# Front order of a Mamba-and-attention block on one core: attention output turned behind the output projection, norms on GpSimd, value copies on VectorE

## What is computed

```python
xn = _layernorm(x)
s = _L0_attn_ref(xn, ...)      # x + mamba2(layernorm(x)), then x + gelu MLP(layernorm(x))
g = _silu(_L0_ffn_ref(xn, ...))
return x + s * g
...
# _L0_ffn_ref, the part that matters here
h = _rms(x, n1_w)
q = _rms(heads(wq), qn_w); k = _rms(heads(wk), kn_w); v = heads(wv)     # 16 heads of 8
ao = softmax(causal(q k^T / sqrt(8))) @ v ... @ wo.T                    # first 32 channels set to 0
x = x + ao
xf = _rms(x, n2_w)                                                      # "second norm"
logits = nan_to_num(xf @ gate_w.T)                                      # 4 experts, the best 2 weighted
return x + weighted sum of four expert MLPs of xf
```

## Time and profile before

| | |
|---|---|
| median of 3 runs (range) | 860.65 us (860.46 to 865.01) |
| the profiled execution: time, span | 861.28 us, 859.5 us |
| granted TensorE clock, mean | 0.993 |
| TensorE matmuls / weight loads busy | 784.9 us (91%) / 482.5 us (56%) |
| VectorE busy | 618.1 us (72%) |
| ScalarE busy | 498.5 us (58%) |
| GpSimd busy | 320.8 us (37%) |

### The profile page before, as it was taken

The page is one execution under the profiler, slowest core; times in us unless marked ns, Lnnn a source line. Parts: engine busy times, 40 slices in busy tenths (PEclk is TensorE's granted clock), DMA queues, the critical chain, the costliest instruction groups (busy, mean ns, idle before and its releaser), DMA issues. The chain is left out here.

```text
span 859.5 us, 18101 instructions
## 1 busy us (share of the span) xinstructions
PE 784.9 (91%) x5472; PEld 482.5 (56%) x5472; DVE 618.1 (72%) x1469; ACT 498.5 (58%) x928; POOL 320.8 (37%) x600
## 2 busy tenths in 40 slices
PE   2779999998999989998999989999899998999897
PEld 1455564755557465665647555475556656475545
DVE  2786479785887768786697858877587876967534
ACT  2435784476753776457844767537764568447552
POOL 5424543053512717036340535227170362505400
PEclk9999999999999999999999999999999999999999
DMA  4000000000000000000000000000000000000000
GB/s 166 2 8 17 12 0 1 9 16 25 0 8 12 14 12 0 8 14 25 0 0 8 14 24 0 6 13 14 12 0 8 13 25 0 0 8 14 24 2 13
DMA packets 15145, 11.73 MB, mean 14 GB/s; under 512 B 1040, under 2 KB 13968, under 8 KB 14992
## 3 DMA queue, kind: packets, MB, share of 16 engines
q1 hardware_dynamic: 15120, 11.43, 4.4%
HBM read 7.76 MB, written 2.10 MB: 11 GB/s over the span
## 5 line engine op out<-in xcount | busy, mean ns | idle before, releaser
L1102 ACT ACTIVATE sb_pr<-S 128x768 f32<-128x768 f32 (+1 forms) x192 | 161.2, 878 | 135.0 <-PE S L445 134.9
L1198 DVE TENSOR_REDUCE sb_mx<-S 128x2 f32<-128x256 f32 (+3 forms) x256 | 198.0, 818 | 32.8 <-PE S L445 31.6
L1722 POOL TENSOR_SCALAR_AFFINE_SELECT sb_pr<-sb_pr 128x256 f32<-128x256 f32 (+1 forms) x192 | 98.8, 520 | 301.7 <-ACT sb_pr L1102 301.0
L445 PE MATMUL R<-sb_pr,sb_va 128*32 128x512 f32 (+3 forms) x1024 | 89.7, 445 | 6.3 <-POOL sb_pr L1722 6.3
L445 PE MATMUL R<-sb_W,sb_pr 128*128 128x96 f32 (+1 forms) x512 | 69.5, 276 | 0.0
L445 PE MATMUL R<-sb_xfT,sb_W 128*128 128x512 f32 x144 | 69.2, 602 | 0.0
L445 PE MATMUL S<-sb_kT,sb_qT 32*128 32x256 f32 (+3 forms) x512 | 56.0, 383 | 14.2 <-DVE sb_mx L1198 10.7
L445 PEld LDWEIGHTS R<-sb_W,sb_pr 128*128 128x128 f32 x512 | 63.5, 192 | 3.8 <-issue 3.5
L445 PEld LDWEIGHTS S<-sb_kT,sb_qT 32*128 32x128 f32 x512 | 27.4, 182 | 67.0 <-DVE sb_mx L1198 59.2
L1432 DVE SCALAR_TENSOR_TENSOR sb_x<-R,sb_wts,sb_x 128x96 f32<-128x96 f32 x128 | 40.6, 317 | 22.8 <-PE R L445 19.4
L445 PE MATMUL S<-sb_qT,sb_kT 32*128 32x256 f32 (+3 forms) x512 | 56.1, 383 | 0.5 <-ACT sb_pr L1102 0.5
(11 more groups left out here) (217 smaller groups left out, 1708.7 us busy)
## 6 DMA issues: line engine op xcount, KB each, us to landing
sb_xin<-x SPq DMA_DIRECT2D x9, 256.0 KB, 2.8
sb_W<-weights SPq DMA_DIRECT2D x1, 2290.0 KB, 11.6
sb_qT<-sb_mT SPq DMA_DIRECT2D x128, 4.0 KB
sb_xres<-x SPq DMA_DIRECT2D x8, 256.0 KB, 2.8
out<-sb_xres SPq DMA_DIRECT2D x7, 256.0 KB, 2.3
sb_cT<-sb_xact SPq DMA_DIRECT2D x8, 128.0 KB, 2.3
sb_W<-weights SPq DMA_DIRECT2D x1, 514.0 KB, 5.6
sb_cst<-consts SPq DMA_DIRECT2D x1, 328.0 KB, 3.1
```

The lines of the kernel that those rows point to most:

```text
L445: return pe.matmul(o, lhsT, rhs, start=start, stop=stop, skip_group_check=True)
L1102: act.activation(pr[:, e % 4, :, 0:n], S[pair_of_exp(e)][:, :, 0:n], ACT.Exp).then_inc(p_sb, 1)
L1198: o = dve.tensor_reduce(mx[:, n // P - 1, g, heads[0]:heads[1] + 1], found[:, :, at_col:at_col + n], AX.X, ALU.max, negate=True)
L1722: pool.affine_select(out=keep, in_=keep, compare_op=ALU.is_ge, fill=0.0, base=0, pattern=pattern, channel_multiplier=-1)\
```

## The change

On TensorE the first `qkv` projection moves to the end of `stage_a`, ahead of the last turn of y; the second goes in front of the output projection; the transposes of `ao` follow the output projection directly, then the third and fourth `qkv`, `wo`, and the x and z projections. The transposes of `xf` go behind all z projections, right ahead of the query and key transposes, and the gate's matmuls between the fourth and the fifth set of these.

On VectorE the value copies arrive (`evac_values`), two of them ahead of x1 and two behind; both norms leave; the sum of squares goes behind x2; the gate's six steps go between the second and the third key copy. On GpSimd both norms arrive: `first_norm` ahead of the multiply of the query weights, `second_norm` behind it. On ScalarE the value copies leave, the first norm's root comes earlier, the squares of x2 are taken in two halves, all z copies go ahead of `x1T` and `xfT`, and the first taps and the gate's exponential go behind the query copies. In the last front (tail alone) the orders stay the same but for the engine of the norms.

```diff
+            def project_qkv(r, t):
+                mm(bank(t)[:, 0:3 * D], xbT[:, t * P:(t + 1) * P], w("qkv")).then_inc(qkv_ps, 1)
+
+            def turn_second_norm(r):
+                pe.wait_ge(xf_sb, at(xf_sb, r, 1))
+                transposes(R[0], lambda t: xf[:, t, :]).then_inc(xfT_ps, 1)
+
+            def gate(r):
+                pe.wait_ge(xfT_sb, at(xfT_sb, r, 1))
+                pe.wait_ge(x1_sb, at(x1_sb, r, T))
+                for t in range(T):
+                    i = mm(R[2][:, t * E:(t + 1) * E], xfT[:, t * P:(t + 1) * P], w("gate"))
+                i.then_inc(gate_ps, 1)
...
+                if head:
+                    project_qkv(r, 1)
+                if tail:
...
                     i.then_inc(op_ps, 1)
-                if head:
-                    pe.wait_ge(xbT_sb, at(xbT_sb, r, 0))
-                    pe.wait_ge(p_sb, at(p_sb, r, 0))
-                    for t in range(T):
-                        mm(bank(t)[:, 0:3 * D], xbT[:, t * P:(t + 1) * P], w("qkv")).then_inc(qkv_ps, 1)
                 if tail:
                     pe.wait_ge(ao3_sb, at(ao3_sb, r, 2))
                     transposes(R[0], lambda t: ao[:, t, :]).then_inc(aoT_ps, 1)
...
                 if head:
-                    project_x(r, 0)
+                    project_qkv(r, 2)
+                    project_qkv(r, 3)
...
                 if head:
+                    project_x(r, 0)
                     project_x(r, 1)
                     project_z(r, 0)
-                    project_z(r, 1)
...
                 if head:
                     project_x(r, 2)
+                    project_z(r, 1)
                     project_z(r, 2)
-                if tail:
-                    pe.wait_ge(xf_sb, at(xf_sb, r, 1))
-                    transposes(R[0], lambda t: xf[:, t, :]).then_inc(xfT_ps, 1)
...
-                if head:
                     project_z(r, 3)
-                if tail:
-                    pe.wait_ge(xfT_sb, at(xfT_sb, r, 1))
-                    pe.wait_ge(x1_sb, at(x1_sb, r, T))
-                    for t in range(T):
-                        i = mm(R[2][:, t * E:(t + 1) * E], xfT[:, t * P:(t + 1) * P], w("gate"))
-                    i.then_inc(gate_ps, 1)
+                if tail and not head:
...
                 if head:
 
                     for n in range(2 * G):
+                        if tail and n == 0:
+                            turn_second_norm(r)
+                        if tail and n == T:
+                            gate(r)
                         if n == 0:
...
                 weigh_values(r, G * UNITS - 2)
+                pe.wait_ge(xbT_sb, at(xbT_sb, r, 1))
+                pe.wait_ge(p_sb, at(p_sb, r, G * UNITS))
+                project_qkv(r, 0)
                 turn_y(r, T - 1)
...
+            def evac_qkv(r, ts):
+                if 0 in ts:
+                    act.wait_ge(rn_sb, at(rn_sb, r, 0))
+                    act.wait_ge(lo_sb, at(lo_sb, r, 0))
+                    act.wait_ge(pv_ps, at(pv_ps, r, 0))
+                for t in ts:
                     act.wait_ge(qkv_ps, at(qkv_ps, r, t + 1))
                     act.activation(qk[:, t].rearrange("p a h d -> p (a h d)"), bank(t)[:, 0:2 * D], ACT.Copy,
-                                   scale=ratio[:, t:t + 1])
-                    act.activation(va[:, t, :, 0:HD],
-                                   bank(t)[:, 2 * D:3 * D].rearrange("p (h d) -> p h d", h=AH),
-                                   ACT.Copy, scale=ratio[:, t:t + 1]).then_inc(qkv_sb, 1)
+                                   scale=ratio[:, t:t + 1]).then_inc(qk_sb, 1)
...
                 if head:
-                    evac_qkv(r)
+                    evac_qkv(r, (0, 1))
                 if tail:
                     act.wait_ge(aoT_ps, at(aoT_ps, r, 1))
                     act.activation(aoT[:], R[0][:, :], ACT.Copy).then_inc(aoT_sb, 1)
                 if head:
-                    act.wait_ge(qkv_sb, at(qkv_sb, r, T))
+                    evac_qkv(r, (2, 3))
+                if head:
+                    act.wait_ge(qk_sb, at(qk_sb, r, T))
                     act.activation(sq[:], qk[:], ACT.Square).then_inc(sq_sb, 1)
+                if tail:
+                    act.wait_ge(ln2_sb, at(ln2_sb, r, 2))
+                    act.wait_ge(x1n_sb, at(x1n_sb, r, 0))
+                    inverse_root(r, mv2[:, :, 1], r2, r2_sb, 1.0, 0)
+                if head:
                     act.wait_ge(conv_dve, at(conv_dve, r, 0))
                     act.wait_ge(conv_pool, at(conv_pool, r, 0))
                     evac_xc(r, 0)
...
-                    inverse_root(r, mv2[:, :, 1], r2, r2_sb, 1.0, 0)
+                    act.wait_ge(x2_sb, at(x2_sb, r, 2))
+                    act.wait_ge(yss_sb, at(yss_sb, r, 0))
+                    for t in range(2):
+                        act.activation(junk[:, t // 2, t % 2 * D:t % 2 * D + D], x2[:, t, :], ACT.Square,
+                                       accum_out=x2ss[:, t:t + 1])
...
                 if tail:
-                    act.wait_ge(x2_sb, at(x2_sb, r, 2))
-                    act.wait_ge(yss_sb, at(yss_sb, r, 0))
-                    for t in range(T):
+                    for t in range(2, T):
                         i = act.activation(junk[:, t // 2, t % 2 * D:t % 2 * D + D], x2[:, t, :], ACT.Square,
                                            accum_out=x2ss[:, t:t + 1])
                     i.then_inc(x2ss_sb, 1)
...
                     evac_z(r, 0)
-                if tail:
-                    act.wait_ge(xfT_ps, at(xfT_ps, r, 1))
-                    act.activation(xfT[:], R[0][:, :], ACT.Copy,
-                                   scale=vec[:, V_N2W:V_N2W + 1]).then_inc(xfT_sb, 1)
+                if head:
+                    evac_z(r, 1)
+                    evac_z(r, 2)
+                    evac_z(r, 3)
+                if tail:
                     act.wait_ge(x1T_ps, at(x1T_ps, r, 1))
                     act.activation(x1T[:], R[1][:, :], ACT.Identity, bias=vec[:, V_LN2B:V_LN2B + 1],
...
-                if head:
...
-                    for n in range(2):
-                        tap = V_CONVW + TAPS * n + TAPS - 1
-                        act.wait_ge(xc_sb, at(xc_sb, r, n + 1))
...
-                        act.activation(cv[:, n], xc[:, n, TAPS - 1:TAPS - 1 + L], ACT.Identity,
...
+                    evac_xf(r)
+                if head:
...
                             act.wait_ge(dt_sb, at(dt_sb, r, 0))
                             act.activation(sp[:, 2], sp[:, 1], ACT.Exp, scale=-1.0).then_inc(spe_sb, 1)
-                            if tail:
-                                gate_exp(r)
-                elif tail:
+                if head:
+                    for n in range(2):
+                        tap = V_CONVW + TAPS * n + TAPS - 1
...
+                        act.activation(cv[:, n], xc[:, n, TAPS - 1:TAPS - 1 + L], ACT.Identity,
+                                       bias=vec[:, V_CONVB + n:V_CONVB + n + 1],
+                                       scale=vec[:, tap:tap + 1]).then_inc(conv_act, 1)
+                if tail:
                     gate_exp(r)
...
+            def evac_values(r, ts_):
+                if 0 in ts_:
+                    dve.wait_ge(rn_sb, at(rn_sb, r, 0))
+                    dve.wait_ge(pv_ps, at(pv_ps, r, 0))
+                for t in ts_:
+                    dve.wait_ge(qk_sb, at(qk_sb, r, t + 1))
+                    ts(va[:, t, :, 0:HD], bank(t)[:, 2 * D:3 * D].rearrange("p (h d) -> p h d", h=AH),
+                       ratio[:, t:t + 1], None, ALU.mult).then_inc(qkv_sb, 1)
...
                     values(r, 3, ot3_ps, ao3_sb)
+                if head:
+                    evac_values(r, (0, 1))
+                if tail:
                     dve.wait_ge(op_ps, at(op_ps, r, 1))
...
+                if head:
+                    evac_values(r, (2, 3))
...
-                if head:
-                    dve.wait_ge(sq_sb, at(sq_sb, r, 1))
-                    dve.tensor_reduce(rqk[:, 0], sq[:].rearrange("p t a h d -> p (t a h) d"), AX.X,
...
                     dve.wait_ge(wo_ps, at(wo_ps, r, 1))
                     tt(x2[:, :, MASKED:D], R[3][:, 0:T * OC].rearrange("p (t c) -> p t c", t=T),
                        xn[:, :, MASKED:D], ALU.add).then_inc(x2_sb, 1)
...
-                    dve.wait_ge(r2_sb, at(r2_sb, r, 2))
-                    dve.wait_ge(x1T_ps, at(x1T_ps, r, 0))
-                    for t in range(T):
-                        i = ts(x1n[:, t, :], x1[:, t, :], mv2[:, t, 0:1], r2[:, 1, t:t + 1],
-                               ALU.subtract, ALU.mult)
-                    i.then_inc(x1n_sb, 1)
-                if head:
+                    pass
+                if head:
+                    dve.wait_ge(sq_sb, at(sq_sb, r, 1))
+                    dve.tensor_reduce(rqk[:, 0], sq[:].rearrange("p t a h d -> p (t a h) d"), AX.X,
+                                      ALU.add).then_inc(ssqk_sb, 1)
...
```

(42 more changed lines are left out.)

49 lines of the change are left out of this document (27 added, 22 removed).

## The result

The changed kernel takes 888.88 us (median of four runs, 887.41 to 891.23) against 862.83 for the kernel before on the same chip (four runs now, 860.46 to 865.05; the three above had 860.65); the ratio is 1.0305 with a 95% interval of 1.0261 to 1.0349. It is slower, as forecast, but by 26 us where I had 18.9, and it lies 0.9 us above my range of 860 to 888. The profiled execution took 887.41 us, with a span of 885.7, at a mean granted clock of 0.980 (0.993 before).

A forecast was written before the change was run, and what follows sets the result against it. TensorE, busy 91%, was taken as the bound, so only its standing still mattered. Per round -0.57 + 0.9 + 0.47 + 1.9 = +2.7 us, times seven +18.9, hence 879.5 us; own range 870 to 887, eight in ten 860 to 888.

The forecast's parts named there:

- the front: Stretch from one round's output projection to the first block of scores; 17.83 us in round 2, seven times in full.
- S: Start of the query and key transposes in the front; 322.37 before, forecast at 322.7 (321.8 to 323.2).
- what follows S: Query and key transposes to first scores: 5.6 us against 5.14, +0.47, contact left out.
- Projections and copies: First projection hidden, taking 0.65 us out of the front; value copies on VectorE 0.28 us each (0.2 to 0.4).
- The first norm on GpSimd: Four steps of 0.33 us (0.28 to 0.77) make 1.3; its transposes start 0.9 earlier, TensorE waiting about 1.5.
- What is queued behind it: GpSimd multiplies query weights (1.27 us) only after the first norm; VectorE's big multiply, needing them, starts 0.5 us later.
- Contact of the second norm with VectorE: GpSimd's norm steps and VectorE's SBUF steps delay each other over a shared port pair: +0.9 us on S.
- a gain of 1.1 us for taking the norm off VectorE: VectorE's chain from big multiply to last subtraction loses the second norm and gap (1.15 us): 3.8 instead of 4.90.
- Contact of the gate with the convolution: The gate's six VectorE steps, beside GpSimd's b2 addition and convolution, end 1.9 us later (1.4 to 2.4).
- the case in which min/max slips in behind is_equal: Among the gate's six steps: the gate ends 1.4 us later in this case, 2.4 otherwise.
- My fourth rival: Granted clock falls to half once more in each front, costing 1 us each: 886.5 us; chance 0.13.
- Ends: First and last fronts differ by under 0.4 us each, opposite in sign, counted as nothing (±0.5).

The follow-up runs named there:

- experiment 8: The kernel before with only its first qkv projection moved ahead of the last turn of y: 857.61 us, ratio 0.9926.
- experiment 3: The changed kernel with twelve tensor_scalar instructions added on GpSimd at its end, VectorE at rest, to price operation pairs at 128 and 512 columns: 889.60 us.
- experiment 5: The changed kernel with the first norm's GpSimd steps as one product each, the mean left out: 876.25 us, ratio 1.0133.
- experiment 11: The changed kernel with the second norm alone back on VectorE, the first staying on GpSimd: 893.87 us, ratio 1.0331.
- experiment 4: The changed kernel with GpSimd's b2 addition and convolution waiting for the gate's sixth step: 883.76 us, ratio 1.0244.
- experiment 12: The changed kernel with six unused products of 256 columns on TensorE in its wait for the first norm: 891.95 us, ratio 1.0318.
- experiment 9: The changed kernel with both norms back on VectorE, and the gate's place and ScalarE's order put back: 876.63 us, ratio 1.0138.
- 10: The kernel before with one projection ahead of the turn of y, and two taps and the gate's exponential behind the query copies: 855.32 us, ratio 0.9892.
- 7: The changed kernel with the first norm alone back on VectorE, plus six unused TensorE products in the wait for it: 884.37 us, ratio 1.0228.
- 14: The changed kernel with norms, gate and ScalarE's order put back, plus nine unused TensorE products in the front's waits: 867.74 us, ratio 1.0063.
- 15: The kernel before with first projection earlier, taps and gate's exponential later, plus three unused TensorE products in the first norm's wait: 852.05 us, ratio 0.9878.
- experiment 1: The changed kernel with both norms back on VectorE, all other moves kept: 880.98 us, ratio 1.0188.
- experiment 13: The changed kernel with the first norm's steps as single products (mean left out) and GpSimd's b2 addition and convolution behind the gate: 881.12 us, ratio 1.0223.

## Why the prediction was right in sign and wrong in size

*The direction* came from the right structure: TensorE waits in the front, and S and what follows S decide. I had +2.7 us a round; the round grew by 3.75. The step that failed is one term, and it was partly covered by another that came out smaller.

*Projections and copies: right.* The first projection is hidden and worth 0.65 us (experiment 8). The value copies take 0.35 us, inside my 0.2 to 0.4. ScalarE's root stands at 322.01 (321.80 + 0.21), 8.13 us behind the turn of yz, where I had 8.16.

*The first norm on GpSimd: the step that failed.* "I take 0.33, near the 16-column row as 128 columns are" against a measured 0.79, beyond even my upper bound of 0.77. I had ordered the rows by columns only. The rows that I took as bounds multiply (and add), or take a maximum and multiply; this step subtracts and multiplies. At 512 columns that pair takes 2072 ns, not 769 (experiment 3), so those rows bounded another operation. Four steps are 3.13 us instead of 1.3, and the start is 0.48 us behind ScalarE instead of 0.3: +2.0 on x1n, and +2.0 on S (17.86 us behind the turn of yz where I had 15.86). Experiment 5 shows it as cause: the cheaper pair alone gives 12.6 us back.

*What is queued behind it: right.* The weights' multiply follows at once (325.59), and VectorE's multiply waits for it, 3.83 us. With this order any delay of x1n goes straight to S.

*Contact of the second norm with VectorE: right in size, and incomplete in kind.* I had +0.9; S lies 0.71 us behind the end of the last subtraction (331.74 against 331.03). The four steps, 0.37 alone, took 4.35 us in all. But I had also booked a gain of 1.1 us for taking the norm off VectorE, 0.2 more than the contact, and by experiment 11 the move as a whole is worth nothing (S 0.16 us later with it, the scores the same).

*Contact of the gate with the convolution: mechanism right, size too large.* I took 1.9, the middle of 1.4 and 2.4; the six steps took 2.4 us instead of 1.13, that is +1.3, the case in which min/max slips in behind is_equal (335.07, between 0.46 and 1.24). Without contact the scores come 1.13 us earlier (experiment 4). From S to the scores it is 6.53 us where I had 7.5. The Trainium skill, page "SBUF — State Buffer", section "Who interferes with whom", has the contact as an exclusive lock; by that rule, the trace agrees, for the step of line 1284 ends within 0.03 us of GpSimd's addition (336.50 against 336.48).

So +2.0 on S and -1.0 behind it make +1.0 a round, the 7.3 us by which the profiled execution (887.4) exceeds my 880.2.

*The clock: the wrong question.* My fourth rival let it fall once in each front, at 1 us each. It fell once in each, and in the changed kernel most of the falls cost nothing, because they hit work that ends inside a wait. Of that kernel's 26 us the clock is not the cause: by its timeline the 1.35 us of waiting behind the fall take it up, and the three fronts of experiment 12 that have no fall have their scores no earlier, but for 0.4 us in round 6. In its neighbours it is a cause: 2.6 us a fall in experiment 9, about 1.9 in 10, and 9.7, 8.9 and 3.3 us came back by the medians when the waits were filled (7, 14, 15), the last the least sure. The kernel before has such falls too, but fewer.

*Ends: wrong, small.* I counted nothing (±0.5) where the trace shows +1.5 and +1.7 us. The first front itself is as I had it: its scores come at 34.09 us instead of 34.07. What makes round 0's output projection late stands behind it: the second projection ahead of it, 0.6 as in every round, and, in this execution, a fall near 65 us that lasts 6.8 us instead of 3.4; the two are read from the timeline and not tested. The last front is longer by the norms on GpSimd. TensorE turns the first norm 8.82 us behind the output projection's start instead of 6.44, and with both norms on VectorE (experiment 1) this front takes 47.22 us, as before (47.23), against 48.90; with the cheaper pair (experiment 5) it takes 47.64. So most of it is the same mis-sized price again. Both are offset by the 3.0 us of falls in the profiled execution of before, so the sum did not show them.

*What the change is worth part by part*, as far as the runs separate it: the first projection -0.65 us a round, the later taps, with the gate's exponential, -0.55 (both shown in the order of before). In the changed kernel, the price of the first norm's steps is +1.76 and the gate's contact +1.13 at the scores; without both they come 2.61 earlier (experiment 13), which leaves 0.49 of the 3.10. With norms, gate and ScalarE's order put back and the waits filled, 867.74 us stay against 852.05 in the order of before. Of these 15.7 us I put 3.9 down to the taps (7 x 0.55, if they are worth the same in this order) and 4.3 to the second projection ahead of the output projection (7 x 0.62, read from its place in the timeline); no run takes either out alone here. The rest, about 1.1 us a round, is left for TensorE's remaining order and the value copies on VectorE; the runs don't separate it.

## What to carry to other kernels

Price an operation that moves to another engine by a row with the same pair of operations on that engine, not only by a row of the same size, or measure it first: one kernel with six lines would have corrected this forecast. Where an engine hands over in the middle of a serial chain, count who stands behind it in both queues. And in a stretch where TensorE waits, watch where the granted clock falls: an edit that shortens the path can move the fall onto it, and a few idle products in the wait can be worth more than the edit.

## What I had not expected of the hardware

- GpSimd's price depends on the pair of operations: at 128 columns 786 ns for subtract and multiply, 441 to 449 for add and multiply or multiply and add with two scalars, 367 with one. At 512 columns 2072 against 769, so each further column costs 3.35 ns ((2072 - 786) / 384) or 0.83 ((769 - 449) / 384).
- In contact the loser may wait for more than one instruction. In round 2 the second norm's last three steps take 1.33 to 1.35 us each instead of 0.37: one beside VectorE's multiply (1.32), one beside its two casts (1.29 for both) and one beside its two subtractions (1.29 for both), and not beside one of a pair (0.69). Each ends 0.16 to 0.24 us behind the multiply or the pair. VectorE's casts take 1.29 as before. In the program VectorE waits for a semaphore at just these three places, and not between the two of a pair.
- A fall of the granted clock to half came to 6.8 us at half clock in experiment 9 (windows of 2 us at 0.73, 0.50, 0.50 and 0.57, each missing share counted twice) and cost 2.6 us there; in the changed kernel it came to 3.4 (0.76, 0.50 and 0.88 from 324 to 330 in round 2) and cost nothing. What sets its length the runs don't show.
